# Second attention: another order of vector and matmul work inside a unit

## The reference, cut to what matters

```python
q = (q_c @ w_qb).reshape(b, s, NH, QK).transpose(0, 2, 1, 3)   # NH = 32, QK = 192
q_rope = q_rope * cos + rotate_half(q_rope) * sin
scores = jnp.einsum('bhqd,bhkd->bhqk', query, key_s) * scaling
attn = jax.nn.softmax(scores, axis=-1)
out = jnp.einsum('bhqk,bhkd->bhqd', attn, v)
return out.transpose(0, 2, 1, 3).reshape(b, s, NH * VD) @ w_o
```

## Time and profile before

| | us |
|---|---|
| runs of the kernel before | 959.36, 961.40, 962.72 (median 961.4) |
| the profiled execution | 959.71 |
| its span | 957.8 |

### The profile page before, as it was taken

One profiled execution on the slowest core, in us unless ns is written; L12 is line 12 of the kernel. 1 busy time (PEld: TensorE's weight loads), 2 busy tenths in 40 slices (PEclk: granted clock), 3 DMA queues, 4 the chain that ended last, 5 costly groups with the idle time before them and its releaser, 6 DMA issues. The chain is left out here.

```text
span 957.8 us, 15142 instructions
## 1 busy us (share of the span) xinstructions
PE 827.3 (86%) x4592; PEld 551.7 (58%) x4592; DVE 687.3 (72%) x1331; ACT 542.9 (57%) x1167; POOL 536.4 (56%) x480
## 2 busy tenths in 40 slices
PE   3699994699996976899999999997999999997476
PEld 1478873577774853466565656564565565654144
DVE  3648887645343645989888989898889898883553
ACT  3667883633323844766666666664666666662233
POOL 1415342011222226989888888895898888872013
PEclk9989997799997987999999999998999999999589
DMA  8350000844422621666666666664666666664101
GB/s 332 120 206 2 1 2 2 225 118 154 142 79 83 193 67 28 167 159 152 153 154 151 155 152 150 156 155 100 148 158 151 155 152 153 152 153 118 60 22 67
DMA packets 91521, 120.86 MB, mean 126 GB/s; under 512 B 30320, under 2 KB 41584, under 8 KB 91440
## 3 DMA queue, kind: packets, MB, share of 16 engines
q1 hardware_dynamic: 66864, 86.31, 32.4%
q10 hardware_dynamic: 24576, 33.59, 14.3%
HBM read 42.22 MB, written 2.10 MB: 46 GB/s over the span
## 5 line engine op out<-in xcount | busy, mean ns | idle before, releaser
L1451 DVE TENSOR_REDUCE nmax<-bank 128x1 f32<-128x512 f32 x256 | 174.1, 680 | 46.6 <-PE bank L1394 44.5
L1527 ACT ACTIVATE prob<-bank,nmax 128x512 f32<-128x512 f32 x172 | 118.4, 688 | 110.6 <-DVE nmax L1451 99.8
L1588 POOL TENSOR_TENSOR prob<-prob,rinv 128x512 f32<-128x512 f32 x129 | 132.6, 1042 | 36.8 <-DVE rinv L1459 34.7
L1392 PE MATMUL bank<-xk_hi,q_hi 128*128 128x512 f32 x256 | 113.1, 442 | 23.4 <-ACT prob L1527 16.2
L1467 DVE STREAM_TRANSPOSE blk<-prob 128x512 f32<-128x512 f32 x172 | 120.2, 699 | 7.3 <-ACT prob L1542 5.8
L1392 PEld LDWEIGHTS bank<-xk_hi,q_hi 128*128 128x128 f32 x256 | 48.3, 189 | 101.2 <-issue 51.8
L1393 PE MATMUL bank<-xk_lo,q_hi 128*128 128x512 f32 x256 | 101.7, 397 | 0.0
L1394 PE MATMUL bank<-xk_hi,q_lo 128*128 128x512 f32 x256 | 100.8, 394 | 0.0
L1583 POOL TENSOR_TENSOR q_lo<-stage_a,q_hi 128x512 fp32r<-128x512 f32 x64 | 82.2, 1285 | 28.3 <-ACT q_hi L1521 28.2
L1579 POOL TENSOR_TENSOR stage_a<-stage_a 128x512 f32<-128x512 f32 x64 | 82.9, 1295 | 7.1 <-DMA stage_a<-stage_a 6.2
L1527 ACT ACTIVATE stage_a<-bank,nmax 128x512 f32<-128x512 f32 x84 | 57.8, 689 | 45.7 <-DVE nmax L1451 39.3
(11 more groups left out here) (240 smaller groups left out, 1980.7 us busy)
## 6 DMA issues: line engine op xcount, KB each, us to landing
pT<-blk SPq DMA_DIRECT2D x256, 64.0 KB, 2.0
pT<-blk ACTq DMA_DIRECT2D x256, 64.0 KB, 2.1
raw_e<-blk SPq DMA_DIRECT2D x256, 64.0 KB, 2.1
raw_e<-blk ACTq DMA_DIRECT2D x256, 64.0 KB, 2.1
raw_e<-in_wo SPq DMA_DIRECT2D x16, 512.0 KB, 3.9
stage_a<-stage_a SPq DMA_DIRECT2D x128, 64.0 KB, 2.0
raw_e<-in_wmod SPq DMA_DIRECT2D x6, 1024.0 KB, 11.1
stage_a<-in_wmod SPq DMA_DIRECT2D x12, 512.0 KB, 4.4
```

The lines of the kernel that those rows point to most:

```text
L1392: pe.matmul(sbk, q_hi[:, u % 2, q], xk_hi[:, 2, ks], start=True, stop=False)
L1451: dve.tensor_reduce(nmax[:, s % RING:s % RING + 1], s_bank[s % 2][:, :], AX.X, ALU.max, negate=True).then_inc(max_done, 1)
L1527: act.activation(prob[s % RING], s_bank[s % 2][:, :], ACT.Exp, bias=nmax[:, s % RING:s % RING + 1], accum_out=rsum[:, s % RING:s % RING + ...
L1588: pool.tensor_tensor(prob[s % RING], prob[s % RING], bc(rinv[:, s % RING:s % RING + 1], [P, S]), ALU.mult).then_inc(norm_pool, 1)
```

## The change

Three orders inside the stage are changed; no instruction is added or taken away.

- `ROPE_AT`: the sine product runs in rounds 1 and 5 (s modulo 4 = 1), not in rounds 0 and 4.
- `OUT_AT`: all four output tiles are made in round 6 in one piece of 12 matmuls, ahead of `scores` of round 7; `o_ps` is signalled once for each couple, and the waits on it are renumbered. In `evict` every tile now waits for the whole piece.
- In VectorE's round 4 the context remainder stands ahead of `turn`.

```diff
-            ROPE_AT = {0: 0, 2: 1}
+            ROPE_AT = {1: 0, 2: 1}
             PV_AT = {1: (0, 1), 3: (2, 3)}
-            OUT_AT = {6: (0, 1), 7: (2, 3)}
+            OUT_AT = {6: (0, 1, 2, 3)}
...
                     def evict(b):
                         for n in range(TPB):
-                            dve.wait_ge(o_ps, 2 * HP * (b + 1) - 1 + n // 2)
+                            dve.wait_ge(o_ps, HP * (b + 1))
...
                             row_inv(s - 2)
-                        if TURN_LAG <= s < ROUNDS + TURN_LAG:
-                            turn(s - TURN_LAG)
-                        if s % TPB in ROPE_AT and s // TPB + 2 < UNITS:
-                            rotate(s // TPB + 2, ROPE_AT[s % TPB])
                         if s % 8 == 4 and 0 <= s // 8 - 2 < COUPLES:
                             j = s // 8 - 2
                             dve.wait_ge(chi_done, j + 1)
                             dve.tensor_tensor(by_block(cT_lo[:, :]), ct_bank[:, :].rearrange("p (g t q) -> p g t q", g=QD, t=TPB),
                                               by_block(cT_hi[:, :].bitcast(F32)), ALU.subtract).then_inc(clo_done, 1)
+                        if TURN_LAG <= s < ROUNDS + TURN_LAG:
+                            turn(s - TURN_LAG)
+                        if s % TPB in ROPE_AT and s // TPB + 2 < UNITS:
+                            rotate(s // TPB + 2, ROPE_AT[s % TPB])
...
                     def out_weights(j):
-                        ge(act, o_ps, 2 * j)
+                        ge(act, o_ps, j)
...
-                            ge(act, o_ps, 2 * j)
+                            ge(act, o_ps, j)
```

## The result

| | kernel before | kernel after |
|---|---|---|
| median of 4 runs each, same comparison | 961.1 us (959.36 to 962.72) | 969.1 us (968.27 to 969.63) |
| the profiled execution | 959.71 | 968.69 |
| its span | 957.8 | 966.8 |

The ratio is 1.0079, with a 95% interval of 1.0064 to 1.0095. The change makes the kernel slower by 8 us. The prediction, 6.5 us faster and at most 963.0, was wrong in sign, and the time lies outside its range.

What follows compares the result with a forecast made beforehand. PE was taken as the bound, with two stops a couple. Terms -8.2 + 0.5 + 1.25 = -6.5 us gave 953.2 from the profiled 959.7, 954.9 on the median 961.4; range 949.5 to 963.

Steps and rivals of the forecast that it cites:

- What bounds the kernel: Steady rounds: PE bounds, stopping twice a couple, 0.25 us ahead of `scores` of round 6, 0.42 ahead of output product.
- The output product's wait: Ahead of the output product: its wait for `cT_lo` goes in 19 couples, with restarts, 8.2 us gained.
- The new stall of `cT_lo`: DVE's round 4: `cT_lo` waits about 0.4 us for `cT_hi`, transpose and row maximum 5 queued behind; nothing charged.
- two margins of under 0.1 us: `scores` 0 and 1: exponentials 6 and 7 arrive 0.08 and 0.05 us early, so PE stays unbroken; nothing charged.
- rival 1: At `scores` 0 and 1, a new wait replaces the old; one place costs up to 6.3 us, both 12.6; chance 0.22.
- Rival 2, late issues: ACT's round 3: SP's queue lengthens issues, more couples get late `cT_hi`, about 0.8 us each; chance 0.12.
- SP's last two moves: nothing there.: SP's queue: last two moves 1.5 to 2.3 us later, context two rounds after their landing, so no cost.
- The start, +0.5: First rounds: sine product falls between row maxima that PE just feeds, nothing to 0.72 us, taken as 0.5.
- The end, +1.25: Last `evict`: first gate product starts 1.4 us later behind six more matmuls, 0.15 comes back, so +1.25 us.
- The `evict` term: Last `evict`: first gate product, now on tile 1, waits behind six more matmuls, 1.4 us later.
- The long issues: ACT issues near 1.44 us in round 3: if instruction fetches cause them, late couples stay as many and the sum stands.

Runs made afterwards that it cites:

- the swap last: The changed kernel with SP's swap behind all eight moves of a unit instead of ahead of the seventh: 965.8 us, ratio 1.0044.
- the last kernel: Kernel before with sine product moved only from round 16 on, and ACT's context rounding ahead of its two round 3 DMA issues: 944.4 us, ratio 0.9829.

## Why the prediction was wrong, step by step

**What bounds the kernel** held: PE does, with its stops ahead of `scores` of round 6 and ahead of the output product. But I priced the first at 0.25 us as a thing that this change leaves alone. It was the one that grew.

**The output product's wait** held in size: -8.2 predicted, -7.7 us of excess gone. But I put it down to the change as a whole. One of the three parts suffices. Of 465.98 us of steady time, the sine product's move takes 6.75; the remainder first adds 12.4 alone, 0.3 on the one piece, 4.7 on the sine product, and 8.6 on sine product and one piece. With the sine product moved there was nothing left for it to remove, since with no sine product in round 4 `cT_lo` ends 0.72 us earlier. I added up three edits as one schedule and never asked what each one did beside the others.

**The new stall of `cT_lo`, "about 0.4 us", charged at nothing.** This is the step that failed. I saw it, and its queue, and I took the two margins of under 0.1 us at `scores` 0 and 1 to absorb it. Measured, the order that makes this stall costs 8.6 us of steady time (469.7 against 461.1 with the transpose first again), where the sum had nothing. What ran differs in two terms. DVE takes 0.73 and 0.72 us for the two steps behind a sine product and a row maximum, where I had reckoned 0.6 for the second (after, rounds 1 and 2, columns as above; this makes the row maxima behind a sine product late, it doesn't lengthen the stall):

```profile
606.46 0.69 DVE L1443 TENSOR_TENSOR stage_a<-bank,stage_a 64x512 f32<-64x512 f32 x1
...
607.72 0.69 DVE L1451 TENSOR_REDUCE nmax<-bank 128x1 f32<-128x512 f32 x1 [0.56 <-PE bank L1394]
608.44 0.17 DVE L1459 RECIPROCAL rinv<-rsum 128x2 f32<-128x2 f32 x1
```

and `cT_hi` starts more than 1.42 us after exponential 3 in 20 of 30 couples instead of 11 (median 1.48, before 1.33), because of ACT issues of 0.8 us where the earlier trace rows has 0.62. By this second term the stall is 0.64 us in the couple shown and 0.72 in the mean, not 0.4. Every row maximum behind it, and with them the exponentials, are late by the difference, and `cT_hi` itself holds exponential 4: +3.4 us ahead of `scores` of round 6. Behind it, **rival 1** came true at one of its two places: `scores` of round 1 restarts in 23 of 29 couples, 2.9 us together with one wait of 1.1. In a row that is a matmul of 0.48 us behind one of 0.39:

```profile
603.75 0.39 PE L1382 MATMUL bank<-xk_hi,w_lo 128*128 128x512 f32 x1
603.97 0.48 PE L1392 MATMUL bank<-xk_hi,q_hi 128*128 128x512 f32 x1
```

I had put its price for one place at up to 6.3 us; at `scores` of round 0 the margin held. The rival was half as dear as thought and still not alone in what went wrong.

**Rival 2, late issues.** Its cause is there in a milder form. It counted couples with issues near 1.4 us: `cT_hi` 1.6 us or more after exponential 3 in 10 couples before and in 10 after. It didn't count delays of 0.2 us, of which there are now 9 more. The rule of the Trainium skill that I named there ("Trainium Kernel Development and Optimization", key constraints: DMAs issued from SP and ACT share 16 engines and interleave) doesn't settle it: the sine product alone has the same SP waits and a median of 1.34 us, as before. The two kernels with sine product and remainder first both, and the swap ahead of the last moves (the changed one and that with two pieces), have 1.48; with the swap last it is 1.33, and sine product and one piece, transpose first, has 1.39. These are medians of one profile each.

The rows of SP's queue say more. Here is the SP issue that runs when ACT's second issue of round 3 starts, before (ACT's starts at 604.38 and takes 0.62 us) and after (611.03, 0.82 us):

```profile
604.05 0.59 SPq L1347 DMA_DIRECT2D pT<-blk  x1
```

```profile
610.90 0.59 SPq L1347 DMA_DIRECT2D pT<-blk  x1
```

I took this pair in all fourteen profiles, leaving out the places where an instruction DMA runs (see below). Where the SP issue has started more than 0.3 us ahead of ACT's, ACT's takes 0.61 us (147 places); at 0.1 to 0.2 us ahead it takes 0.76 in the median (25), within 0.1 us 0.82 (12). So the change shifted the two queues against each other: the distance is 0.33 us in nearly all couples before, and 0.02 to 0.14 us in about half of them after. No run moves this distance alone.

**"SP's last two moves: nothing there."** This failed. Their context does wait for landings in the changed kernel, where before none did in the steady stretch: ahead of the context half of round 1 at 447.24, 511.37 and 800.94 us, which make the 3.3 us that the table has more. The view of line L1405, and one such place:

```profile
  DMA raw_e<-blk: 2.9, 3
```

```profile
445.04 1.40 ACTq L1347 DMA_DIRECT2D pT<-blk  x1
...
447.24 1.08 PE L1405 MATMUL bank<-raw_e,c_all 128*64 128x512 f32 x4 [1.02 <-DMA raw_e<-blk]
```

In all three it is SP's very last move of the couple that lands last: issued at 443.54, 507.17 and 797.86 us, it takes 3.6, 4.1 and 2.9 us to land, where the page has 2.1. The last landing of SP's moves lies 3.0 us ahead of the context half in the median before, 1.1 with the sine product alone and 0.6 after, so one slow landing now shows. With the swap last it lies 3.9 us ahead; there is 1 wait left, of 1.2 us, for a move that ACT issued, and the steady stretch is 4.4 us shorter. I had a margin of two rounds, and took it as a reason to stop looking, without the landing times.

**The start, +0.5.** It was +2.2 us. I bounded the sine product's place from 0 to 0.72. In round 4 it had covered a time in which DVE waits for PE anyway. Moved to round 5, DVE idles first and is then late:

```profile
379.05 0.69 DVE L1451 TENSOR_REDUCE nmax<-bank 128x1 f32<-128x512 f32 x1 [0.44 <-PE bank L1394]
379.91 0.71 DVE L1467 STREAM_TRANSPOSE blk<-prob 128x512 f32<-128x512 f32 x1 [0.17 <-POOL prob L1588]
380.65 0.69 DVE L1443 TENSOR_TENSOR stage_a<-bank,stage_a 64x512 f32<-64x512 f32 x1
...
383.03 0.77 PE L1392 MATMUL bank<-xk_hi,q_hi 128*128 128x512 f32 x1 [1.28 <-ACT prob L1527]
383.59 0.63 PE L1393 MATMUL bank<-xk_lo,q_hi 128*128 128x512 f32 x1
```

PE was idle for 1.28 us, and behind that its matmuls take 0.63 us and step by 0.43 instead of 0.23: the clock is at the lower of its two levels. The same place by stretches, before first, then after:

```profile
380.00:386.00 6.00, 4.58 (x17) 1.00 0.56 134
```

```profile
382.00:388.00 6.00, 4.97 (x14) 0.72 0.54 131
```

That the sine product's place is the cause is shown by the last kernel, where putting it back for 16 rounds takes 2.4 us off this stretch. The 2.2 us have two parts. Sine product and remainder first, two pieces, has the same stops of PE here (1.01 and 1.28 us), but its granted clock stays at 1.00 and rounds 0 to 16 take 33.4 us: 1.2 us more than before, for the place alone. The other seven profiles with the sine product in round 1 from the start all show a lower clock here and take 34.3 to 34.7 us, so some 1.0 us is the clock. Why that one kept it is open.

**The end, +1.25.** It was +2.35. The `evict` term was right: it waits 3.17 us where the earlier trace rows has 1.75, 1.4 us more.

```profile
896.89 2.50 DVE L1473 TENSOR_TENSOR bank<-bank,gate 128x512 f32<-128x512 f32 x4 [3.17 <-PE bank L1421]
```

The other 1.1 us I didn't think of: `scores` of round 255 itself stands behind six more matmuls (its row maximum comes 6.05 us behind that of round 252, before 4.65), and in the last couple there is nothing later to make up for it, so its exponential and transpose are later too. That this makes the 1.1 us is argued: in four pairs of kernels that differ by the one piece only, this end is longer by 2.3, 0.9, 2.5 and 2.5 us.

**The sum again.** Steady, from the table of excess steps: -7.7 + 3.4 + 2.8 + 1.5 + 3.3 + 0.2 = +3.5, against +3.7 measured between the row maxima. With +2.2 and +2.35 at the ends, the change costs 8.2 us, and the medians say 8.0. The failed step is 8.6 us of the 14.5 between forecast and result, not all of it: sine product and one piece, without the stall, is still slower than before (963.3, ratio 1.0032), because its steady gain is 4.9 us instead of 8.2 and its two ends cost 6.0 instead of 1.75.

**The long issues.** The prediction named instruction fetches as a possible reason for issues near 1.4 us. The DMA records of the traces bear on it: the page lists DMAs of kind "instruction" on queue q8, and those of 16 KB cover 4% of the time of rounds 16 to 252. In the fourteen profiles, 285 issues of block moves or swaps on ACT and SP in these rounds took 1.1 us or more, and every one of them lies beside such a DMA; so do two of the three slow landings above (those of 3.6 and 4.1 us). ACT has 10 of them before and 10 after, as many as late couples. Not every issue beside such a DMA is long. That they go together is shown; that the fetch makes the issue long is not, since no run moved one.

**Left open.** Why the third landing took 2.9 us; whether the 16 KB DMAs are the cause of the long issues or share one with them; and why one kernel of eight kept its clock at the start.

## What to carry to other kernels

When a change reorders several things at once, cost each part alone and each with the others before summing: here one part did the whole job, and a second, aimed at the same wait, only added a wait of its own. Moving an instruction forward in a queue gained nothing here while what it waits for stayed where it was: look first at the producer, and where the producer is an activation behind DMA issues on the same engine, try it ahead of them (with the sine product's move, 13 us of 960 here; without that move only 1.9 us of steady time). And look at what each wait leaves to the next: the same reorder cost 12.4, 0.3, 4.7 or 8.6 us, depending on what stood around it. A margin smaller than the scatter of the rows that it is made of is no cover; charge it.

## What the runs showed of the hardware

- On ACT an activation that stands ahead of a DMA issue in program order doesn't delay it: the issue starts at 605.49, 0.02 us after the activation, and both run side by side. In the other order the activation waits for the whole issue (0.75 us idle, put to "issue").
- DVE's step from the start of one 512-column instruction to the next depends on its neighbours: into and out of the 64-partition sine product 0.72 to 0.73 us, and 0.72 again for a row maximum that follows it (but 0.61 for `cT_lo` there, in the kernel before); elsewhere in these rounds mostly 0.57 to 0.65. Moving such a product moves its neighbours by another 0.1 us.
- PE stops of 1.00 and 1.28 us at the start of the stage were followed by a granted clock of 0.72 over 6 us and steps of 0.43 us; in the kernel before, stops of 1.16 and 0.45 us at the same place were followed by a clock of 1.00 and steps of 0.23 to 0.24. In sine product and remainder first, two pieces, stops of 1.01 and 1.28 us were followed by 1.00 too, so these stops alone don't decide it.
- A DMA issue on ACT is longer when one on SP started shortly ahead of it: it takes 0.61 us when SP's started over 0.3 us earlier (147 places), and 0.76 to 0.82 in the median when it started less than 0.2 us earlier (37 places).
- All 285 issues of 1.1 us or more in rounds 16 to 252 of fourteen profiles lie beside an instruction DMA of 16 KB on q8.
